# Turning a kernel's last stage to columns, and its delta blocks to even and odd heads in turn

## The reference

```python
# block 0, mixer: conv, silu, then 8 heads of 64 with a spiking membrane
mem = DECAY * mem + dt;  spike = (mem > THR);  mem = mem - spike * THR
alpha = sigmoid(at + asp * spike)          # per step and key channel
# delta rule, state s (64 x 64 per head), gated by alpha and beta
o_t = q_t @ s_t                            # after s decays and takes the new k, v
y = rms(o per head) * head_norm @ Wo
y = sigmoid(gate(h)) * y + h;  z = rms(y) * ff_norm
y = y + (silu(z @ Wff1) * (z @ Wff3)) @ Wff2;      x = x + gate * y
x = x + gate * (gelu(mod(norm(x)) @ w1 + b1) @ w2 + b2)
# block 1: attention over windows of 32 (16 heads of 8), then a quantized layer
x = x + gate * (window_attention(mod(norm(x))) @ wo)
h = mod(norm(x));  n = norm(h) * gamma + beta
x = x + gate * (h + 0.5 * (silu(n @ fc1 + b) @ fc2 + b))
```

## Time and profile before

| | us |
|---|---|
| median of the runs | 1766.11 |
| the profiled execution | 1767.83, span 1766.1 |
| TensorE busy | 1225.7 (69% of the span) |
| its weight loads | 1025.8 (58%) |
| VectorE busy | 1149.0 (65%) |
| ScalarE busy | 562.0 (32%) |
| GpSimd busy | 195.3 (11%) |
| mean granted TensorE clock | 0.778 of 2.4 GHz |

### The profile page before, as it was taken

How to read it: one execution, slowest core, us unless ns; L and a number is a source line. 1 busy time by engine, 2 the same in 40 slices (tenths; PEclk the granted TensorE clock), 3 DMA queues, 4 the chain that set the end, 5 groups by cost and what they waited for, 6 DMA issues and landing times. The chain is left out here.

```text
span 1766.1 us, 26022 instructions
## 1 busy us (share of the span) xinstructions
PE 1225.7 (69%) x8836; PEld 1025.8 (58%) x8836; DVE 1149.0 (65%) x3533; ACT 562.0 (32%) x927; POOL 195.3 (11%) x189
## 2 busy tenths in 40 slices
PE   1210002699888998888988889878758578678685
PEld 1100001488777887777877778777338357456374
DVE  4798987867788777887777877751235444363353
ACT  3110000343344442434424344322333343343321
POOL 2000002110111101111101111010101010020000
PEclk8565555698899999999999999965676777687666
DMA  2000000000000000000000000001000000000000
GB/s 69 0 1 1 1 1 1 1 1 0 0 0 0 0 0 0 0 0 0 0 0 0 0 0 0 1 1 31 26 0 1 1 7 1 0 7 1 0 7 6
DMA packets 9466, 7.28 MB, mean 4 GB/s; under 512 B 2872, under 2 KB 7547, under 8 KB 9406
## 3 DMA queue, kind: packets, MB, share of 16 engines
q1 hardware_dynamic: 7886, 5.07, 1.0%
q10 hardware_dynamic: 1520, 1.48, 0.3%
HBM read 5.50 MB, written 1.05 MB: 4 GB/s over the span
## 5 line engine op out<-in xcount | busy, mean ns | idle before, releaser
L775 PEld LDWEIGHTS ps<-delta_kq_up,delta_arena 64*128 64x128 f32 x1024 | 122.6, 261 | 64.2 <-ACT delta_kq L530 37.3
L775 PE MATMUL ps<-delta_kq_up,delta_arena 64*128 64x128 f32 x1024 | 129.3, 365 | 36.5 <-ACT delta_kq L530 36.5
L1113 DVE TENSOR_TENSOR delta_tm<-delta_tm,ps 128x256 f32<-128x256 f32 x96 | 40.4, 421 | 157.5 <-PE ps L815 157.5
L872 PE MATMUL ps<-ones,beta_b 1*128 1x1 f32 x8 | 1.8, 346 | 195.5 <-PEq L339 195.5
L872 PEld LDWEIGHTS ps<-ones,beta_b 1*128 1x128 f32 x8 | 1.8, 323 | 196.3 <-issue 196.3
L616 ACT ACTIVATE delta_xf<-ps 128x256 f32<-128x256 f32 (+1 forms) x128 | 48.9, 382 | 204.6 <-PE ps L802 140.3
L815 PE MATMUL ps<-delta_tt,delta_xf 128*128 128x64 f32 x768 | 106.6, 284 | 0.0
L813 PE MATMUL ps<-delta_xf,delta_tt 128*128 128x64 f32 x768 | 106.6, 284 | 0.0
L802 PEld LDWEIGHTS ps<-delta_tm,drive 128*128 128x128 f32 x768 | 95.6, 201 | 17.1 <-DVE delta_zb L964 9.2
L500 POOL TENSOR_TENSOR delta_km<-delta_beta_k,delta_arena 128x512 f32<-128x512 f32 x16 | 32.5, 2034 | 655.2 <-DVE delta_beta_k L1010 655.2
L802 PE MATMUL ps<-delta_tm,drive 128*128 128x64 f32 x768 | 98.5, 284 | 6.2 <-ACT delta_tm L606 6.2
(11 more groups left out here) (360 smaller groups left out, 3086.4 us busy)
## 6 DMA issues: line engine op xcount, KB each, us to landing
out<-x SPq DMA_DIRECT2D x4, 256.0 KB, 2.4
setup_wmod<-in_L_wmod ACTq DMA_DIRECT2D x2, 384.0 KB, 3.8
post_wff<-in_L_attn_Wff SPq DMA_DIRECT2D x3, 256.0 KB
post_w<-in_L_ffn_w SPq DMA_DIRECT2D x2, 256.0 KB
post_fc_q<-in_L_ffn_fc_q SPq DMA_DIRECT2D x2, 256.0 KB
setup_wspike<-in_L_attn_Wspike ACTq DMA_DIRECT2D x1, 256.0 KB
wq<-in_L_attn_Wq ACTq DMA_DIRECT2D x1, 256.0 KB
wk<-in_L_attn_Wk SPq DMA_DIRECT2D x1, 256.0 KB
```

The costliest lines, as they stand in the source:

```text
L775: ins = eng.matmul(m.ps[:, at + n, P * (h // 2):P * (h // 2) + P], up_lift[s][ks, cs], m.kq_up[s][ks, :, half], start=True, stop=True)
L1113: eng.tensor_tensor(v, v, m.ps[:, 6 + n, 0:256].rearrange("p (b s) -> p b s", s=s), ALU.subtract).then_inc(vector_back, vec.one(f"TX{x}{s}"))
```

## The change

- In `spike_phase`, TensorE transposes the 16 tiles of `x` and of `h`, and ScalarE copies them back in place, so that both lie by columns: channels on the partitions, 2048 tokens beside one another.
- In `delta_phase`, `base` and `blocks` issue even and odd heads in turn. `seen_by_q` and `state2` swap operands, so that the output has value channels on the partitions; `output` copies 64 partitions by 512 elements twice instead of 128 by 256 twice. One wait of TensorE ahead of `seen_by_q` goes.
- In `post_phase`, everything stays by columns. `contract` (4 products of 512 columns) takes the place of `back_to_rows` (16 or 20). Sums of a norm become products with a matrix of ones, of 1/128, or with `bd` (ones per head), 512 columns wide, whose result stands in every partition; Ln and Exp then run 512 wide (`mix_root`, `win_root`, `y_logs`, `y_roots`). Gates, scales and shifts are scalars per partition, which merges steps of VectorE. The biases of `w2` and `fc2` go onto `x` on ScalarE (`mix_bias`, `win_bias`); shift and beta go into b1 and fc1_b, `head_norm` into `wo`, once. `rows_out` turns each finished group back with four transposes and a copy ahead of its store.
- The orders of the engines are rewritten to suit; the rest of the diff is names of steps.

```diff
+        @block.tensor
+        def _(eng):
+            for k in range(8):
+                src = (m.x, m.h)[k // 4]
+                for n in range(4):
+                    ins = eng.transpose(m.ps[:, k, P * n:P * n + P], src[:, 4 * (k % 4) + n, :], m.ident[:, :])
+                ins.then_inc(turned, 1)
...
+                eng.wait_ge(turned, k + 1)
+                eng.activation(dst[:, 4 * (k % 4):4 * (k % 4) + 4, :].rearrange("p n d -> p (n d)"), m.ps[:, k, :], ACT.Copy).then_inc(columns, 1)
...
-                eng.activation(y[:, :, :, 0:HD], m.ps[:, 6, 0:256].rearrange("p (c v) -> p c v", c=NP).unsqueeze(2), ACT.Copy)
-                eng.activation(y[:, :, :, HD:P], m.ps[:, 7, 0:256].rearrange("p (c v) -> p c v", c=NP).unsqueeze(2), ACT.Copy).then_inc(scalar_back, act.one("out"))
+                for e in range(2):
+                    ks = slice(HD * e, HD * e + HD)
+                    ins = eng.activation(y[ks], m.ps[ks, 6 + e, :].rearrange("p (c t) -> p c t", c=NP).unsqueeze(2), ACT.Copy)
+                ins.then_inc(scalar_back, act.one("out"))
...
+                    for j in range(2):
+                        for e in range(2):
+                            ks, cs = head(base_heads(n + e)[j])
+                            ins = eng.matmul(m.ps[:, (n + e + 1) % 4, 256 * j:256 * j + 256], m.km[ks, cs], m.kq_base[ks, :, cs], start=True, stop=True)
+                            if j:
+                                ins.then_inc(tensor_back, pe.one(f"base{n + e}"))
...
+                    for h in range(H):
+                        ks, cs = head(h)
+                        half = slice(HD * (h // 2), HD * (h // 2) + HD)
+                        ins = eng.matmul(m.ps[:, at + h % 2, P * (h // 2):P * (h // 2) + P], up_lift[s][ks, cs], m.kq_up[s][ks, :, half], start=True, stop=True)
+                        if h >= H - 2:
+                            ins.then_inc(tensor_back, pe.one(f"up{s}{HALVES[h % 2]}"))
...
+                    o = m.ps[ks, 6 + h % 2, cs]
+                    ins = eng.matmul(o, m.state[ks, h // 2, :], m.kq_all[ks, 1, cs], start=(h < 2), stop=False)
...
+                    ins = eng.matmul(m.ps[ks, 6 + h % 2, cs], m.u_rows[:, HD * h:HD * h + HD], m.a_qk[:, h, :], start=False, stop=(h >= H - 2))
...
-                eng.wait_ge(vector_back, vec.at("XTb32", i))
...
+            def mix_root(p, i, eps):
+
+                bank = {"z": 6, "n1": 6, "n2": 7}[p]
+                eng.wait_ge(mix_tensor, mpe.at("zs" if p == "z" else f"{p}_var", i))
+                eng.activation(m.r_a[:, :], m.ps[:, bank, :], ACT.Ln, scale=1.0 / D, bias=m.eps[:, eps:eps + 1]).then_inc(mix_scalar, mact.one(f"{p}_ln"))
...
+            def y_logs(i, pair):
+                for c in range(2 * pair, 2 * pair + 2):
+                    eng.wait_ge(mix_tensor, mpe.at(f"ys{c}", i))
+                    eng.activation(m.y_sq[:, GT * c:GT * c + GT], m.ps[:, 6 + c % 2, :], ACT.Ln, scale=1.0 / HD, bias=m.eps[:, 1:2]).then_inc(mix_scalar, mact.one(f"y_ln{c}"))
...
+            def mix_bias(i):
...
+                eng.activation(cols(m.xT, i), cols(m.xT, i), ACT.Identity, bias=m.gate_s[:, 2, 0:1]).then_inc(mix_scalar, mact.one("xb"))
...
+            def rows_out(i):
+                eng.wait_ge(win_tensor, wpe.at("rows", i))
+                if i:
+                    eng.wait_ge(stored, 16 * i)
+                eng.activation(m.rows[:, :, :].rearrange("p n d -> p (n d)"), m.ps[:, 5, :], ACT.Copy).then_inc(win_scalar, wact.one("rows"))
+
...
+            def contract(bank, w, src, done, value):
+
+                for c in range(4):
+                    ins_ = eng.matmul(m.ps[:, bank, :], w[:, c, :], src[:, c, :], start=(c == 0), stop=(c == 3))
                 ins_.then_inc(done, value)
...
+            def y_sums(i, pair):
+
...
+                    eng.matmul(m.ps[:, 6 + c % 2, :], m.bd[:, :], m.y_sq[:, GT * c:GT * c + GT], start=True, stop=True).then_inc(mix_tensor, mpe.one(f"ys{c}"))
...
+            def z_sum(i):
+                eng.wait_ge(mix_scalar, mact.at("z_sq", i))
+                eng.matmul(m.ps[:, 6, :], m.ones[:, :], m.sq_a[:, :], start=True, stop=True).then_inc(mix_tensor, mpe.one("zs"))
...
+            def mix_mean(p, i):
+                eng.wait_ge(mix_vector, mvec.at("x1" if p == "n1" else "x2", i))
+                eng.matmul(m.ps[:, 7 if p == "n1" else 6, :], m.mean_w[:, :], cols(m.xT, i), start=True, stop=True).then_inc(mix_tensor, mpe.one(f"{p}_mean"))
...
+            def mix_var(p, i):
+                eng.wait_ge(mix_scalar, mact.at(f"{p}_sq", i))
+                eng.matmul(m.ps[:, 6 if p == "n1" else 7, :], m.ones[:, :], m.sq_a[:, :], start=True, stop=True).then_inc(mix_tensor, mpe.one(f"{p}_var"))
...
+            def scales():
+
+                eng.wait_ge(rest_in, 16 * len(rest_loads))
...
+                eng.matmul(m.ps[:, 1, :], m.ones[0:1, :], m.fc2_s[:, :], start=True, stop=True).then_inc(pre_tensor_done, pre_pe.one("scales2"))
+                for f in range(NF):
+                    ins_ = eng.matmul(m.ps[:, 2, f:f + 1], m.w1[:, P * f:P * f + P], m.mod_cols[:, 0, 3:4], start=True, stop=True)
+                ins_.then_inc(pre_tensor_done, pre_pe.one("b1"))
...
+            def rows_out(i):
+
+                eng.wait_ge(win_vector, wvec.at("x4", i))
+                for n in range(GROUP):
+                    ins_ = eng.transpose(m.ps[:, 5, P * n:P * n + P], m.xT[:, GT * i + P * n:GT * i + P * n + P], m.ident[:, :])
+                ins_.then_inc(win_tensor, wpe.one("rows"))
...
                 if mix:
-                    rows_in(j)
+                    gate_in(j)
                 if i == -1:
-                    eng.wait_ge(rest_in, 16 * len(rest_loads))
-                    eng.matmul(m.ps[:, 0, :], m.ones[0:1, :], m.fc1_s[:, :], start=True, stop=True).then_inc(pre_tensor_done, pre_pe.one("scales1"))
-                    eng.matmul(m.ps[:, 1, :], m.ones[0:1, :], m.fc2_s[:, :], start=True, stop=True).then_inc(pre_tensor_done, pre_pe.one("scales2"))
+                    scales()
                 if win:
                     scores(i, 1)
+                if mix:
+                    y_sums(j, 0)
+                if win:
                     weights_to_columns(i, 0)
                     scores(i, 2)
+                if mix:
+                    y_sums(j, 1)
+                if win:
                     values(i, 0)
                     weights_to_columns(i, 1)
                 if mix:
-                    y_columns(j, 0)
-                    y_columns(j, 1)
+                    gate(j)
                 if win:
                     scores(i, 3)
                     own(i, 0)
                     values(i, 1)
-                if mix:
-                    y_columns(j, 2)
-                    y_columns(j, 3)
-                    gate(j)
-                if win:
                     weights_to_columns(i, 2)
                 if mix:
                     project(j)
...
-                    first_norm_columns(j)
+                    mix_mean("n1", j)
+                if win:
+                    win_mean("n3", i)
+                if mix:
+                    mix_var("n1", j)
+                if win:
+                    win_var("n3", i)
+                if mix:
                     gelu_hidden(j)
                 if win:
-                    fourth_norm_columns(i)
+                    win_mean("n4", i)
+                    win_var("n4", i)
                 if mix:
                     gelu_out(j)
                 if win:
                     last_hidden(i)
                 if mix:
-                    second_norm_columns(j)
+                    mix_mean("n2", j)
+                    mix_var("n2", j)
                 if win:
                     last_out(i)
                 if mix:
                     projections(j)
...
+            def mix_centre(p, i):
+                eng.wait_ge(mix_tensor, mpe.at(f"{p}_mean", i))
+                eng.tensor_tensor(m.xc_a[:, :], cols(m.xT, i), m.ps[:, 7 if p == "n1" else 6, :], ALU.subtract).then_inc(mix_vector, mvec.one(f"{p}_cen"))
...
+                eng.tensor_tensor(m.y_a[:, :], m.y_a[:, :], m.ps[:, 6, :], ALU.add).then_inc(mix_vector, mvec.one("y2"))
                 eng.wait_ge(mix_vector, mvec.at("y2", i))
-                eng.tensor_tensor(y_a, y_a, mod_row(0, 2), ALU.mult).then_inc(mix_vector, mvec.one("y2g"))
-                eng.wait_ge(mix_vector, mvec.at("y2g", i))
-                eng.tensor_tensor(xs, xs, y_a, ALU.add).then_inc(mix_vector, mvec.one("x1"))
-                eng.wait_ge(mix_vector, mvec.at("x1", i))
+                eng.scalar_tensor_tensor(x, m.y_a[:, :], m.mod_cols[:, 0, 2:3], x, ALU.mult, ALU.add).then_inc(mix_vector, mvec.one("x1"))
...
+            def first_norm(i):
+                eng.wait_ge(mix_scalar, mact.at("n1_r", i))
+                eng.scalar_tensor_tensor(m.hT_a[:, :], m.xc_a[:, :], m.mod_cols[:, 0, 4:5], m.r_a[:, :], ALU.mult, ALU.mult).then_inc(mix_vector, mvec.one("n1_nrm"))
```

436 lines of the change are left out of this document (195 added, 241 removed).

## The result

The changed kernel takes 1697.5 us (median of 4 runs, 1696.1 to 1701.1) against 1766.0 us (4 runs, 1763.1 to 1768.1): ratio 0.9616, 95% interval 0.9595 to 0.9638. It is 68.5 us faster, 3.9%. The prediction was 1727 us with a range of 1700 to 1752: the sign was right, the gain was 29 us larger than forecast, and the time lies 2.5 us under the range. The profiled execution took 1701.1 us, its span 1699.3.

The account below looks back on a forecast made before the run. Bounds by phase: VectorE in membrane, VectorE then TensorE in delta chunks, half-clock engine chains in stages. Terms -12.8 - 1.2 - 32.1 + 6 + 0.6 = -39.5 us gave 1727 us, range 1700 to 1752.

Parts of the forecast that it names:

- early part of a stage: Overlapped stages: `rows_out` transposes ahead of the scores cost +0.5 us; head norm taken as 0, bounds -2 and +6.
- stretch from the last hidden product to the end of `fc2`: Stage tail: to `fc2` 9.2 us instead of 10.8, -1.5; `fc2` 3.4 to 6.8 instead of 7.0, -0.2 to -3.6.
- delta blocks: Delta phase: even/odd alternation saves 0.85 us a chunk at levels 32 and 64 only; 15 chunks, 12.8 us, bounds 0 and 21.
- Turned output, rows in the membrane phase: `state2` product 0.9 us instead of 1.87, ScalarE copies +0.9, hidden in chunks 0 to 14; membrane transposes and copies cost nothing.
- end of the last chunk: Last delta chunk, where nothing covers the turned product: 1.2 us gained, bounds 0 and 2.
- First stage: TensorE's norm sums wait behind `scales`, delaying `project` 7.8 to 11.2 us; some 3.5 come back: +6, bounds +2 and +10.
- z norm: Overlapped stages: wide sum queues behind window work and Ln/Exp take 512 columns; +2.3 us a stage, 1.4 to 4.
- Tail: Overlapped stages, `mixed` through `fc2`: 13.5 us saved a stage with the clock between its levels, bounds 8.9 and 18.9.
- `mixed` to gelu: Tail step from `mixed` to the first gelu product: 7.8 us instead of 10.0, -2.2.
- eight wide records: 3.4 at full, 6.8 at half: `w2` and `fc2` in the tail: eight wide records replace 10.8 and 7.0 us; `w2` saves 4.0 to 7.4 us.
- rival A: Clock recovers as new means and variances fill TensorE's gaps; 8 us more per stage, 1703 us, chance 0.20.
- Rivals B, C and D: B: delta period unchanged, 1740 us, 0.16; C: stages all half clock, 1752, 0.11; D: slower, 1782, 0.05.

Follow-up runs that it names:

- filled_gaps: Kernel before, with 3, 2 and 2 unread wide products put into TensorE's three tail waits of an overlapped stage; 1779.3 us.
- bias_full_rows: Kernel before, with each bias record of w2 and fc2 using all 128 weight rows instead of one; 1736.9 us.
- scales_later: Changed kernel, with the first stage's quantisation-scale and folded-bias products behind the head norm's four sums on TensorE; 1688.0 us.
- filled_after: Changed kernel, with four unread wide products more per overlapped stage in short TensorE waits; 1683.1 us.
- filled_three: three_orders with the four fillers of filled_after in the overlapped stages; 1659.1 us.
- filled_full_rows: Kernel before, with the edits of filled_gaps and bias_full_rows together; 1741.1 us.
- the bias runs: Kernel before, with the bias records of w2 and fc2 left out (1734.0 us) or given all 128 weight rows (1736.9 us).
- halves_in_after: Changed kernel, with base and upper delta blocks back in the old order, one half then the other; 1713.0 us.
- only_late_levels: Changed kernel, with only upper blocks of levels 32 and 64 alternating even and odd, the other blocks in old order; 1698.3 us.
- sums_before_z: Changed kernel, with VectorE's row sums and scaling of window 2 ahead of the z norm's scale; 1688.5 us.
- both_orders: Changed kernel, with the new orders of scales_later and sums_before_z together; 1678.4 us.
- three_orders: both_orders, plus the first pair of z products ahead of values(3) on TensorE; 1673.2 us.
- one_row_added: Changed kernel, with w2 and fc2 in four slices and a one-weight-row product into an unused bank behind each; 1716.5 us.

## Why the prediction was right or wrong

The sign and most steps held; the gain was 29 us too small, and three terms of the sum account for 26 of them. The early part of a stage, put at 0.5 us with the head norm at nothing, gave 2.9 us a stage. The stretch from the last hidden product to the end of `fc2`, put at -1.5 and -0.2 to -3.6, gave 6.4. The delta blocks, put at 0.85 us a chunk, gave 1.1 in the steady ones and 4.9 in the first. What the sum had wrong behind the second of these is the account of `w2` and `fc2`, told under "Tail".

**Delta blocks.** Right in mechanism and place, low in size. Levels 32 and 64 carry it, the early levels and the base products nothing, the turned product nothing, and 32 alternating records start within 1.78 us at full clock as forecast. Spread product to `tt`: 10.05 to 10.5 us in the steady chunks against 11.4, so 0.9 to 1.35 and not 0.85. The sum priced the records at full clock, on the ground that the half clock ends at its time anyway; they ran mostly at half clock, where the 32 take 3.8 us instead of 5.0. The rest of the 7 us is the first chunk, 62.0 us before and 57.2 after, 3.9 of it between spread product and `tt` (14.1 and 10.2): I priced 15 chunks by the steady one and didn't look at the first. That part is not surely the order's. It is 14.1 us at a granted clock of 0.56, and in the old order it took 10.2 too where the clock was higher (0.82 in filled_gaps and bias_full_rows, first chunks of 58.2). The old order has first chunks of 60.9 to 62.1 us in four of its six profiles, the alternating order of 57.2 to 58.2 in all twelve.

**Turned output, rows in the membrane phase.** As forecast: 1.09 us for the product (I took 0.9), 2.14 us for the two copies where 1.28 was, both hidden. By the rule of the Trainium skill that the prediction weighed (TensorE: Matmul & The Clock Gate, section on packing small matmuls) the product would have passed its former 1.87 us, as the prediction read it; the trace doesn't agree, it took 1.09. For the rest, the first base product starts between 325.8 and 329.5 us in all kernels here, turned rows or not. The end of the last chunk gained 2.0 us, the bound.

**First stage.** Right in kind and nearly in size, +8.2 for +6: the gated product came 11.1 us later, by the chain that was named, 2.9 of the 3.5 forecast came back up to q, and scales_later took the delay away.

**z norm.** Right in kind, low: +3.7 a stage for 2.3, inside the bounds of 1.4 and 4. VectorE's window sums behind z, which the sum named, were the late item, and TensorE's values(3) at half clock the price.

**Tail.** `mixed` to gelu, 7.9 us for 7.8 forecast. w2 lies in its bounds too (-6.0 to -6.4 of 4.0 to 7.4), but for a reason I didn't give. The step that failed in mechanism is "eight wide records: 3.4 at full, 6.8 at half" as an account of 10.8 and 7.0 us, with the clock left to chance between its levels. The width did next to nothing (0.14 us); the one-row bias records cost 2.3 us a product at full clock (5.90 against 3.57), and in the old w2 also the rise of the clock. Full rows alone take 4.4 us from gelu and w2 and 3.2 from the last hidden layer and fc2 in a stage of the old kernel. The second of these is a large part of why the last stretch, last hidden to the next q, gave 6.4 us a stage and not 3.4: the last hidden products now ran at full clock (3.6 us for 5.15), and fc2 did in two of three stages.

**Early part.** Forecast +0.5 a stage, measured -7.3, -3.6 and +2.3. So the step that put it at 0 failed by 8.6 + 1.5 = 10 us, the largest single miss. By its reason the head norm's products would cost what the VectorE reduction gives back; measured is a stretch that follows the clock, 38.7 us at 0.74 before (43.6 at 0.64 in the first stage), and in the changed stages 36.3 at 0.81, 35.1 at 0.85 and 41.0 at 0.71. The same code took 33.4 to 41.0 us in the stages of these kernels. This is rival A's ground. It had the right consequence (the clock recovers, 1703 us) with a chance of 0.20, and its reason, that means and variances fill TensorE's gaps, is half borne out: filled_after and filled_three show that added work in the short waits of the changed kernel raises the clock of w2, filled_gaps and filled_full_rows that it does not shorten the old tail, and the bias runs show the part that no rival named. Rivals B, C and D are out: chunks of 53.5 us, a clock of 0.81 to 0.87, and 68 us faster.

**Still open:** why a given stage gets 35.1 or 41.0 us for its early part, and with it how much of the 8.6 us the wide sums gave and how much the clock. The half clock lay on it from 1523.2 to 1547.1 in the slow one; no run here changed that stretch alone. It is not random from run to run: the third stage has 41.0 us in the change, halves_in_after, only_late_levels and scales_later, the second in sums_before_z, both_orders and three_orders.

## What to carry to other kernels

Read a chain on TensorE at both clocks before pricing an edit by records: a row that is all at half clock (10.75 us at 0.50) asks why the clock doesn't rise there. In this kernel products with one row of weights inside a group were one cause; a bias can be folded into the residual, a constant or an activation instead. And when a norm is moved from one engine to another, write down what stood behind it in each queue: window sums behind z and quantisation scales ahead of the norm's sums cost this change 19 us that two moves gave back.

## What the runs showed of the hardware that was not expected

- A pair of records with one weight row takes 0.42 us at full clock, a pair with 128 rows over the same 128 columns 0.22; the full-row slice ahead of the one-row pair takes 1.08 us, ahead of the other 0.90. Two one-row products in succession cost no more than full-row ones (1.12 and 1.02 us over 512 columns).
- Reached at half clock, w2 with one-row records stayed at half for all its 10.75 us in every overlapped stage of the kernel before and in one of one_row_added; in the other two, and in fc2 of the kernel before, the clock rose within (0.83). With full rows, or without the bias, it rose within w2 each time (0.71 and 0.67).
- 32 records of 128 columns and 8 of 512 take nearly the same time, 3.57 and 3.43 us at full clock.
- Adding idle products made the changed kernel 14 us faster (one of its four runs was no faster) and the kernel before 17 us slower.
- The order even, odd of 64-row blocks issues a record each 57 ns at full clock (31 of them in 1.78 us), one half after the other 82 ns; at half clock the 32 take 3.79 and 4.96 us.
